# Second expert product of a decoder layer: the contraction of 176 cut in 128 and 48 rows instead of 88 and 88, with both parts of the 48 stacked, so that a tile takes five matrix products in place of six

## What is computed

```python
h1 = jnp.einsum('btd,edc->btec', x, w1_routed)      # 16 experts, d = 256, c = 176
h2 = jnp.einsum('btd,edc->btec', x, w3_routed)
h3 = jax.nn.silu(h1 * h2)
experts_out = jnp.einsum('btec,ecd->bted', h3, w2_routed)
routed_out = jnp.einsum('bted,bte->btd', experts_out, router_probs)
```

## Time and profile before

| | |
|---|---|
| device time, median of 3 runs | 904.76 us (896.44, 904.76, 906.59) |
| profiled execution | 898.93 us, its span 896.8 us |
| PE busy | 700.3 us (78%), 4330 products |
| DVE busy | 596.4 us (67%) |
| POOL busy | 529.8 us (59%) |
| ACT busy | 393.7 us (44%) |
| mean granted TensorE clock | 0.911 of full speed |

### The profile page before, as it was taken

The page is one execution under the profiler, slowest core; times in us unless marked ns, Lnnn a source line. Parts: engine busy times, 40 slices in busy tenths (PEclk is TensorE's granted clock), DMA queues, the critical chain, the costliest instruction groups (busy, mean ns, idle before and its releaser), DMA issues. The chain is left out here.

```text
span 896.8 us, 19120 instructions
## 1 busy us (share of the span) xinstructions
PE 700.3 (78%) x4330; PEld 589.3 (66%) x4330; DVE 596.4 (67%) x1833; ACT 393.7 (44%) x1051; POOL 529.8 (59%) x419
## 2 busy tenths in 40 slices
PE   0777777775405799988997754999999999898993
PEld 0556665664303567655775433899999999898993
DVE  4799999999202666554564464777777777576672
ACT  0644435352003555444542233655555555454451
POOL 0587877776300036666567671667677756764875
PEclk9988979798856999998998885999999999999997
DMA  6701111000296224433223453567677767676874
GB/s 198 248 26 41 54 35 47 29 23 19 72 302 112 71 82 150 157 128 127 104 104 122 144 187 101 95 113 132 121 126 128 125 115 126 110 131 101 132 124 54
DMA packets 86893, 99.04 MB, mean 110 GB/s; under 512 B 10401, under 2 KB 81633, under 8 KB 86753
## 3 DMA queue, kind: packets, MB, share of 16 engines
q0 software_dynamic: 26736, 37.64, 23.2%
q1 hardware_dynamic: 48971, 51.68, 19.9%
q10 hardware_dynamic: 11094, 8.65, 4.1%
HBM read 49.57 MB, written 52.95 MB: 114 GB/s over the span
## 5 line engine op out<-in xcount | busy, mean ns | idle before, releaser
L1412 POOL DMA_INDIRECT out_dram<-yw,xg x143 | 223.3, 1561 | 127.0 <-issue 59.1
L1008 POOL DMA_INDIRECT xs_scratch<-rows,slot x128 | 128.2, 1002 | 78.7 <-DMA xs_scratch<-rows,slot 50.1
L1305 PE MATMUL cbank<-w,stc_hi 88*128 x572 | 116.0, 295 | 1.4 <-DVE stc_lo L1377 0.5
L1305 PE MATMUL cbank<-w_hi,xtc_hi 128*128 x286 | 106.5, 372 | 0.6 <-DVE xtc_lo L1317 0.3
L1305 PEld LDWEIGHTS cbank<-w,stc_hi 88*128 88x128 f32 x572 | 90.3, 190 | 14.3 <-issue 9.2
L1305 PE MATMUL cbank<-w,xtc_hi 128*128 x286 | 94.0, 329 | 0.0
L1305 PE MATMUL cbank<-w_hi,xtc_lo 128*128 x286 | 93.6, 327 | 0.0
L455 PE MATMUL ps_o<-ident,pv 128*128 128x128 f32 x288 | 48.6, 328 | 54.9 <-ACT ot L291 50.1
L1397 DVE TENSOR_SCALAR yw<-cbank,xg 128x256 f32<-128x256 f32 x143 | 69.0, 483 | 29.1 <-PE cbank L1305 16.3
L1317 DVE TENSOR_TENSOR xtc_lo<-cbank,xtc_hi 128x256 fp32r<-128x256 f32 x143 | 60.6, 423 | 36.9 <-ACT xtc_hi L1312 26.2
L455 PEld LDWEIGHTS ps_o<-ident,pv 128*128 128x128 f32 x288 | 40.4, 170 | 63.7 <-POOL pv L256 42.8
(11 more groups left out here) (191 smaller groups left out, 1722.8 us busy)
## 6 DMA issues: line engine op xcount, KB each, us to landing
xg<-xs_scratch SPq DMA_DIRECT2D x143, 144.0 KB
x_in<-x_dram SPq DMA_DIRECT2D x32, 128.0 KB
w_hi<-ctx_t_dram SPq DMA_DIRECT2D x8, 512.0 KB, 3.6
x_scratch<-u SPq DMA_DIRECT2D x32, 128.0 KB
w_hi<-x_scratch SPq DMA_DIRECT2D x8, 512.0 KB
out_dram<-w SPq DMA_DIRECT2D x16, 256.0 KB
w<-w1r_dram ACTq DMA_DIRECT2D x2, 1408.0 KB
w<-w3r_dram ACTq DMA_DIRECT2D x2, 1408.0 KB
```

The lines of the kernel that those rows point to most:

```text
L1008: nc.gpsimd.indirect_dma_start(t["xs"], bass.IndirectOffsetOnAxis(ap=slot[:, n % 2, k:k + 1].bitcast(U32), axis=0), rows[:, n % NROW, k // ...
L1305: last = nc.tensor.matmul(out, stationary, moving, start=j == 0, stop=j == len(pairs) - 1)
L1412: nc.gpsimd.indirect_dma_start(t["out"], bass.IndirectOffsetOnAxis(ap=xg[:, p, ID:ID + 1].bitcast(U32), axis=0), yw[:, p % YB, :], None, c ...
```

## The change

`w2` is read in the order of its rows: rows 0 to 127 as one block of 128 partitions, and rows 128 to 175 (48 of them) twice, at partitions 0 to 47 and 64 to 111 of the second block; the partitions between are filled with zeros from the constant array `pads`. This makes nine DMAs in place of six in `load_weights`, and the wait of `split_hi` counts nine. `sg_` writes the last 48 columns twice, at columns 128 and 192 of a buffer of 256, in a second instruction; the gaps are set to zero once by POOL. `s_t` transposes 128 and 128 columns in place of 88 and 88. `s_lo_` becomes two instructions: the low part of the first 128 rows into `stc_lo`, and the low part of the 48 in place into partitions 64 to 111 of `stc_hi`. `y_mm` takes three products over 128 rows, then one over 112 rows that gives high by high and low by high together, then one over 48 rows for high by low.

```diff
--- before.py
+++ after.py
@@ -34,6 +34,8 @@
 HC = HID // 2
+REST, HALF = HID - P, P // 2
+BOTH = HALF + REST
 CLIP = 54
@@ -1093,15 +1095,19 @@
-        def load_weights(eng, k):
-
-            if k < 4:
+        def load_weights(eng):
+
+            s_w = keep["s_w"]
+            for k in range(4):
                 r, ch = ("w1r", "w3r")[k // 2], k % 2
                 eng.dma_start(keep["w13"][:, ch, :, (k // 2) * HID:(k // 2 + 1) * HID],
-                              t[r].rearrange("e (c p) h -> c p e h", p=P)[ch, :, :, :]).then_inc(keep["s_w"], 16)
-            else:
-                eng.dma_start(keep["w2"][0:HC, 1, k - 4, :, :].bitcast(F32),
-                              t["w2r"].rearrange("e (c p) d -> c p e d", p=HC)[k - 4, :, :, :]).then_inc(keep["s_w"], 16)
+                              t[r].rearrange("e (c p) h -> c p e h", p=P)[ch, :, :, :]).then_inc(s_w, 16)
+            raw, w2r = keep["w2"][:, 1, :, :, :].bitcast(F32), t["w2r"].rearrange("e p d -> p e d")
+            zeros = t["pads"][0:NE * (HALF - REST), 0:D].rearrange("(p e) d -> p e d", e=NE)
+            eng.dma_start(raw[:, 0, :, :], w2r[0:P, :, :]).then_inc(s_w, 16)
+            for at in (0, HALF):
+                eng.dma_start(raw[at:at + REST, 1, :, :], w2r[P:HID, :, :]).then_inc(s_w, 16)
+                eng.dma_start(raw[at + REST:at + HALF, 1, :, :], zeros).then_inc(s_w, 16)
@@ -1120,7 +1126,7 @@
                     f["bp_mm"].wait(eng, n)
-                    eng.wait_ge(keep["s_w"], 16 * 6)
+                    eng.wait_ge(keep["s_w"], 16 * 9)
                     for e in experts:
@@ -1186,8 +1192,7 @@
         def _(eng):
-            for k in range(6):
-                load_weights(eng, k)
+            load_weights(eng)
             eng.wait_ge(s_w, 16 * pre.LOADS)
@@ -1248,15 +1253,15 @@
         hh = sb("hh", [P, 2, HID])
-        sg = sb("sgc", [P, 2, HID])
-        st_hi, st_lo = sb("stc_hi", [HC, 2, 2, P], R32), sb("stc_lo", [HC, 2, 2, P], R32)
-        w2_hi, w2_lo = w2[0:HC, 0, :, :, :], w2[0:HC, 1, :, :, :]
+        sg = sb("sgc", [P, 2, 2 * P])
+        st_hi, st_lo = sb("stc_hi", [P, 2, 2, P], R32), sb("stc_lo", [P, 2, P], R32)
+        w2_hi, w2_lo = w2[:, 0, :, :, :], w2[:, 1, :, :, :]
         yw = sb("yw", [P, YB, D])
...
         f = {n: Flow(sem("fc_" + n)) for n in ("t", "t_hi", "t_ev", "h", "h2", "hh", "sg", "st", "st_hi", "st_ev", "y", "y_ev")}
-        s_hi, s_lo = sem("sc_hi"), sem("sc_lo")
+        s_hi, s_lo, s_zero = sem("sc_hi"), sem("sc_lo"), sem("sc_zero")
@@ -1298,7 +1303,7 @@
         def s_tr(p):
-            return R[4 + p % 2][0:HC, 0:2 * P].rearrange("p (c n) -> p c n", c=2)
+            return R[4 + p % 2][:, 0:2 * P].rearrange("p (c n) -> p c n", c=2)
@@ -1354,16 +1359,19 @@
             f["st"].wait(eng, n - 2)
-            f["sg"].sig(nc.scalar.activation(sg[:, p % 2, :], hh[:, p % 2, :], ACT.Silu))
+            if n == 0:
+                eng.wait_ge(s_zero, 1)
+            nc.scalar.activation(sg[:, p % 2, 0:P], hh[:, p % 2, 0:P], ACT.Silu)
+            f["sg"].sig(nc.scalar.activation(sg[:, p % 2, P:2 * P].rearrange("p (t h) -> p t h", t=2)[:, :, 0:REST],
+                                             hh[:, p % 2, P:HID].unsqueeze(1).to_broadcast([P, 2, REST]), ACT.Silu))
...
             f["st_ev"].wait(eng, n - 2)
-            for half in range(2):
-                last = nc.tensor.transpose(R[4 + p % 2][0:HC, half * P:(half + 1) * P], sg[:, p % 2, half * HC:(half + 1) * HC],
-                                           ident[:, :])
-            f["st"].sig(last)
+            out = s_tr(p)
+            nc.tensor.transpose(out[:, 0, :], sg[:, p % 2, 0:P], ident[:, :])
+            f["st"].sig(nc.tensor.transpose(out[:, 1, :], sg[:, p % 2, P:2 * P], ident[:, :]))
@@ -1374,8 +1382,10 @@
             f["st_hi"].wait(eng, n)
-            f["st_ev"].sig(nc.vector.tensor_tensor(st_lo[:, p % 2, :, :], s_tr(p), st_hi[:, p % 2, :, :].bitcast(F32),
-                                                   ALU.subtract))
+            f["y"].wait(eng, n - 2)
+            nc.vector.tensor_tensor(st_lo[:, p % 2, :], s_tr(p)[:, 0, :], st_hi[:, p % 2, 0, :].bitcast(F32), ALU.subtract)
+            f["st_ev"].sig(nc.vector.tensor_tensor(st_hi[HALF:BOTH, p % 2, 1, :], s_tr(p)[HALF:BOTH, 1, :],
+                                                   st_hi[HALF:BOTH, p % 2, 1, :].bitcast(F32), ALU.subtract))
@@ -1385,8 +1395,10 @@
             f["y"].sig(accumulate(R[6 + p % 2][:, 0:D], [
-                (x[:, p % 2, half, :], w[:, half, bass.ds(e, 1), :]) for half in range(2)
-                for x, w in ((st_hi, w2_hi), (st_hi, w2_lo), (st_lo, w2_hi))]))
+                (x, w[:, bass.ds(e, 1), :]) for x, w in (
+                    (st_hi[:, p % 2, 0, :], w2_hi[:, 0, :, :]), (st_hi[:, p % 2, 0, :], w2_lo[:, 0, :, :]),
+                    (st_lo[:, p % 2, :], w2_hi[:, 0, :, :]), (st_hi[0:BOTH, p % 2, 1, :], w2_hi[0:BOTH, 1, :, :]),
+                    (st_hi[0:REST, p % 2, 1, :], w2_lo[0:REST, 1, :, :]))]))
@@ -1441,6 +1453,7 @@
         def _(eng):
+            nc.gpsimd.memset(sg[:, :, P:2 * P], 0.0).then_inc(s_zero, 1)
             run(eng, "g")
```

## The result

| | before | after |
|---|---|---|
| device time, median | 901.31 us (4 runs, 896.44 to 906.59) | 917.51 us (4 runs, 912.83 to 920.44) |
| profiled execution | 898.93 us | 920.44 us |
| scatter 8 begins | 585.24 | 598.72 |
| scatter 140 begins | 887.16 | 908.59 |

The ratio is 1.0189, with an interval of 1.0142 to 1.0236: slower by more than 1%, and 12.5 us over the 905 us forecast. The two profiled executions lie further apart (21.5 us) than the medians (16.2 us), because that of before is one of its quicker runs and that of after its longest. The granted clock is alike (0.911 and 0.916).

What follows compares the result with a forecast made beforehand. POOL's scatters were taken to bound the expert phase from scatter 8 on. PE's saving 0, splits 2.4 and DMAs 0.6 gave 3.0 us: 901.9 on the profiled execution, 905 as median, range 893 to 916.

Steps and rivals of the forecast that it cites:

- POOL sets the end of the kernel before: Expert phase: from scatter 8 on POOL's scatters, 2.27 us each on average, set the end, so PE's saving is worth 0.
- less than 1.6 us after its result: Test on the kernel before: no scatter after number 8 starts this soon, so results have 1.6 us of cover.
- Rows of contraction (112 and 48 in place of 88) ... are put at nothing, since PE has the spare time of this saving: PE's products and transposes per tile: changed shapes cost 0, while one product fewer takes the tile from 2.13 to 2.01 us.
- The later chain: Iterations after the first 16, `hh` to `hh`: 1.77 us plus 0.25 gives 2.02, under POOL's 2.27, so worth 0.
- Rival D: PE's tile: the change saves less than claimed because transposes grow or the 112-row product is slower; its share is in A.
- A: The forecast itself: POOL keeps the end, 3.0 us slower, 901.9 us on the profiled execution; chance 0.77.
- The splits: First 16 iterations: two instructions for one cost 0.15 us on ACT (10 times), 0.10 on DVE (9 times): 2.4 us, 1.7 to 4.1.
- Nine DMAs: Start of the cross phase: nine weight DMAs for six hold ACT's first `Exp` 0.6 us longer, 0.4 to 1.0.
- Rival C: Start of the cross phase: longer issue on ACT holds `Exp` 9.8 us, giving 911.1, or 13.5, giving 914.8; chance 0.14.
- Rival B: Expert phase: scatters follow results, so PE's saving of 15.2 us comes through, giving 886.7 us; chance 0.09.
- `Exp` within 1 us: Sign at the start of the cross phase: ACT's first `Exp` stays within 1 us of 268.40.
- more results than scatters: Sign in mid-phase: scaled results get further ahead of scatters than 88 to 83, up to the 8 that `yw` allows.

Runs made afterwards that it cites:

- e8: The kernel before with the last of its six products in `y_mm` left out: 896.99 us, ratio 0.9976.
- e1: The changed kernel with its fifth product over 112 rows in place of 48: 909.51 us, ratio 1.0131 to the kernel before.
- e9: The changed kernel with the fifth product over 112 rows and one SiLU of 256 columns in place of two: 908.52 us, one run.
- e4: The changed kernel with DVE's second subtraction over all 128 partitions into its own buffer, in place of 48 partitions in place: 920.02 us, one run.
- e7: The changed kernel with the two DMAs of zeros replaced by one GpSimd memset, leaving seven DMAs: 921.96 us, one run.
- e5: The kernel before with all six weight DMAs issued by SyncE after its first cross phase loads, none by ACT: 882.80 us, ratio 0.9834.
- e12: The kernel before with all six products over 64 of the 88 rows: 920.69 us, one run.
- e3: The kernel before with the last of its six products over 64 of the 88 rows: 923.15 us, ratio 1.0273.
- e11: The kernel before with the last of its six products over 72 of the 88 rows: 897.47 us, one run.
- e10: The changed kernel with DVE's second subtraction kept at 48 partitions but written into its own buffer: 923.38 us, one run.
- e2: The changed kernel with three of its nine weight DMAs (second copy, both zeros) issued by SyncE: 923.35 us, ratio 1.0282.

## Why the prediction was wrong

**POOL sets the end of the kernel before: right.** e8 shows it from one side and e1 from the other: with the tile under 2.27 us hardly a scatter waits for its result after the first eight (24 in before, 24 and 32 in e8, none in e1). The prediction's test, "less than 1.6 us after its result", missed number 24, though: it reads eight counts first and begins 3.32 us after its result, where 3.24 is the least, so the cover there was 0.1 us and not 1.6.

**"Rows of contraction (112 and 48 in place of 88) ... are put at nothing, since PE has the spare time of this saving": this step failed.** I compared it with nothing, and gave it the 0.12 us of all others without the bounds that I gave elsewhere. It took 0.28 us more with the border behind it, the transposes 0.05 more, so the tile went to 2.34 and not to 2.01. (Nor would 2.01 have come with 112 rows. The later chain, put at 2.02, measures 2.12 from `hh` to `hh` right behind the splits in e1, and 2.06 in e9 with its one SiLU; e1's tile is 2.12. Both are under 2.27.) The trace of before could have warned me. It has 32 products over 16 rows, in the cross phase:

```profile
365.50 1.45 PE L747 MATMUL bank<-w_hi,xwq 128*128 128x512 f32 x3
366.88 0.42 PE L921 MATMUL bank<-identb,th 16*128 16x16 f32 x4
```

```profile
366.88 0.32 PEld L921 LDWEIGHTS bank<-identb,th 16*128 16x128 f32 x4 [0.76 <-issue]
```

Three products of 512 columns at their usual 0.43 us would end at 366.79; the first over 16 rows begins 0.09 later, together with its weight load. I had also named the point from which it would matter (2.27) for the other chain only. Price: 8.0 us (after less e1 by the medians; 7.9 by the traces from scatter 8 to 83). Rival D, "the end would be A's", was wrong for the same reason: PE did less than nothing, and the end was not A's. The Trainium skill, "TensorE: Matmul & The Clock Gate", section "LDWEIGHTS (loading the stationary operand)", says that a weight load over 32 rows takes as long as one over 128. The rows agree (0.18 us over 64, 0.19 over 72); the time is lost in when the load begins.

**The splits: the mechanism right, the term too small, 4.7 us for 2.4.** ACT's part was the 0.15 us that I had, and SiLU to `split_hi` came out at 0.38 for 0.41. DVE's was 0.28 for 0.10, over my upper bound of 0.17, which assumed that lack of overlap was the worst that a split could bring and charged it to one instruction. e4 gives the 0.40 us that I predicted for two subtractions, for 128 partitions; the one over 48 lost the overlap on both its sides, 0.61. It was paid in 10 to 11 iterations, 10 x 0.44 + the last, where I took 9 and 10. By the Trainium skill's fixed latencies ("VectorE: DVE Perf Modes", TRN2 errata) the estimate was 3.5 us in sum, nearer than mine, but with 0.13 on DVE and 0.23 on ACT; the trace has 0.28 and 0.15.

**Nine DMAs: the place right, the term too small, 4.6 us for 0.6.** I assumed that a larger remainder (3700 packets) would be allowed once 16 engines share it, so that only 130 more had to pass first. The remainder shrank to 1986, so 1844 more had to pass; that they went at 340 a us, faster than the 130 to 300 that I had, kept the price at 4.6. e7 puts 3.3 us on the zeros. From the Trainium skill, "DMA: Bandwidth & Descriptors", section "Why a DMA increments its semaphore by 16 and not by 1", by which a DMA is spread over 16 engines or 11, I had worked out that ACT would be free at the same time. The time speaks against that use of the rule, not against the rule, since it says nothing of how long a packet takes. Rival C had this mechanism, sized 9.8 and deciding "from about 6 us on": it was 4.6, and not enough alone. Its direction came true with two others beside it. That all of the 4.6 us reach the end is argued, not shown: the delay of `Exp` passes on in full to the first scores (5.2 us later), but e7 gave back 3.3 and shows nothing of it in its one time, and e5's 26 us became 16.

**The sum.** 4.6 + 4.7 + 8.0 = 17.3 us, to compare with 16.2 of the medians (12.8 to 21.3 by the interval). Since the 8.0 is itself a difference of medians, the independent test is the rest: without it the sum is 9.3, and e1 measured 8.2 over the 901.31 (8.9 over the kernel before beside it). So A as forecast, 3.0, would have been 8 to 9 even with 112 rows. Rival B had no part in it.

**What would show it.** Of the signs named, `Exp` within 1 us, `hh` to `hh` 2.78, result 7 some 3 us later, the tile of 2.01 to 2.05 and more results than scatters all came out otherwise (4.2, 2.97, 12.8 with the cross phase in it, 2.34, none). Only SiLU to `split_hi` was near. POOL's stops at the sixteen changes of expert and at 8 and 24 stayed, but smaller ones were added where a result or a count came late (32, 48, 56, 64, 72, 80 and 136). "The forecast is wrong if scatters begin right after their results in mid-phase" is what happened.

**Left open.** Why packets of the small DMAs take 0.15 us; how much of the later `Exp`, and of the nine DMAs' data, reaches the end; where between 64 and 72 rows the edge lies; whether it is the weights or the product that PE holds back (the Trainium skill, "TensorE: Matmul & The Clock Gate", section "Step-by-step: what each phase is for", says that loads are pulled ahead where the row groups don't conflict or where they go to a background buffer; it gives no number of rows at which that changes, and no run here tests it); and why the cross phase wanders by up to 8.6 us.

## What to carry to other kernels

Price an instruction by a row of its very shape, partitions and rows of contraction above all, and give it bounds if there is none: "less work" in a product made the tile longer. An engine with spare time is only cover up to the pace of the one that sets the end, here 0.14 us a tile. And look at who is held by an issue of DMAs before tuning their number: moving them to a queue for which nobody waits at that point was worth 16 us to the kernel before.

## What the runs showed of the hardware

- PE: passing between products over 48 or 64 rows and products over 88 to 128 costs 0.09 to 0.10 us at each border and up to 0.10 in the instructions behind it, 0.33 us a tile in e12, e3 and (against the 2.01 worked out) the changed kernel. Into products over 16 rows it is 0.09 too (366.88 in the trace of before). A product over 72 rows costs nothing (e11), and among themselves 64-row products take the usual 0.12 us.
- DVE: successive instructions over 128 partitions overlap by 0.08 us. Next to one over 48 partitions (64 to 111) they don't: 0.29 and 0.33 us for 0.20 and 0.20 (e10, e4).
- DMA: an engine that issues is held until most of the data ahead has passed, also data that another engine issued (e2: 17.28 us for 13.40). The 1 KB packets of the 128-partition DMA pass at 340 a us; those left after the small DMAs of 48 and 16 partitions take 0.15 us each, where those of the earlier trace rows, from 88 partitions, take 0.09 (0.665 x 16 x 21.65 us / 2550), and in both cases only 120 to 130 pass in a us.
